# Audio tower, one core: fewer VectorE instructions in each unit, new step orders, and more hats in the first two units

## The chip, the cores and the metric
One Trainium2 chip; the program runs on one of its cores. The time is that of the device in microseconds (us), the median of several runs of one launch. Engines: TensorE (PE), VectorE (DVE), ScalarE (ACT), GpSimd (POOL) and SyncE (SP), which issues DMAs.

## The reference
128 batches of x, 750 positions by 64 channels in float32, pass three layers.
- Tokens: x is cut into 46 windows of 16 positions (taps). A product with w_off gives two offsets for each window and tap, dy and dx. With px = 16 w + k + dx, x0 = floor(px), frac = px - x0:
```
wy  = max(0, 1 - |dy|)
val = wy * ((1 - frac) * x[x0] + frac * x[x0 + 1])      # 0 outside of x
tok = val @ w_def + b_def, a class token ahead of it, + positional encoding   # 47 x 128
```
- Attention: softmax(Q K'/sqrt(128) + est) V on the layer norm of the tokens, where est = W2 tanh(W1q q + W1k k + b1) for each pair, added to the tokens.
- Experts: on the second layer norm, the two best of 8 (softmax gates, renormed) and a shared one, each relu(x w1 + b1) w2 + b2, added again. The output is 128 x 47 x 128.

## The kernel before, in words
A unit is 8 batches; there are 16. The interpolation between rows is computed in two ways. Six batches of a unit are gathered: VectorE makes row indices (stage_a, L535), GpSimd issues 36 indirect DMAs of 128 rows each into G (gathers, L367, 12 for each of three pairs of batches), and VectorE multiplies them with the weights and adds (combine, L588, pieces c0 to c2). The last two go by hats: ScalarE computes max(0, 1 - |px - row|) for all rows (hats, L402; half a batch is three Abs and one Relu; pieces h0 to h3 and k0 to k3, two to a half), TensorE multiplies this with the rows of x as they lie in memory (dense, L798, pieces n0 to n3 on TensorE) and VectorE multiplies by wy (dense_out, L618, n0 and n1 on VectorE). Both end in VT, of which TensorE makes the tokens with w_def (b3, L770).

Positions and wy of the hats must lie on all partitions. SyncE writes them to the DRAM buffer pw (write_positions, p0), reads them back spread out (spread_positions, q0: PXB and WYB), and loads the plain rows XN (load_rows, y0). It also loads x (x0, in 16 pieces), passes the estimates of the attention through DRAM into SC (e0, e1, e2) and stores the result (d9).

Each engine is a queue with an order written out by hand: ORDER lists the pieces of a step, AHEAD says which unit a letter works on. In step s the letters m and e work on unit s, r on s - 1, f, g, d (experts up, spread weights, weighted and down) on s - 2, n, c, b, k on s + 1, h on s + 2, a, p, q, y on s + 3 (offsets: a3 and a4), t and x on s + 4 (transposes of x, t0 to t3). A step ends about where stage_a writes the indices. early() runs single pieces for the units ahead of step -1; after the constants and VectorE's setup, steps -1 to 4 are unrolled, the middle is a loop of two steps, the rest is unrolled. On VectorE, chain() makes an instruction wait for the end of the one before.

Around the change: rstd (L562) takes 1/sqrt by a shifted start and three Newton steps, on 94 x 4 numbers; m6 (L656) the maximum of the scores (piece r6 in the order); m13 (L684, r13) ranks the gates by comparing all pairs; b3 on VectorE (L632) takes the tokens out of the bank to h0, for which the next unit's a3 waits, because both use bank 0. m8 (r8) adds the attention, m12 (r12) gates, m14 (r14) their weights, m51 and m52 the estimates, d8 adds up the experts, d9 transposes the output.

Of the kernel before, what the change touches and what calls it, by code (L numbers as in the profile page):

```python
# [6 lines left out]
K = 16  # L7
W = L // K
# [4 lines left out]
UNITS = B // NB  # L13
LP = 768
# [82 lines left out]
def audio_tower(nc, x, consts, rows, pw, est, out):  # L97
# [4 lines left out]
    with ctx:  # L102
# [21 lines left out]
        ones = sb("ones", [128, 128])  # L124
# [12 lines left out]
        offs = sb("offs", [128, NBLK, 8])  # L137
        nw = sb("nw", [128, NBLK, 4])
        rr = sb("rr", [128, GBLK, 4])
        e01 = sb("e01", [128, GBLK, 4, 2])  # L140
        e01f = e01[:, :, :, :].rearrange("p t n s -> p (t n s)")
        rowb = sb("rowb", [128, GBLK])
        idx = [sb(f"idx{p}", [128, GBLK * 4], i32) for p in range(2)]
        aw = [sb(f"aw{p}", [128, GBLK, 4, 2]) for p in range(2)]
# [13 lines left out]
        Z2 = [sb(f"Z2{p}", [128, COLS]) for p in range(2)]  # L158
# [13 lines left out]
        h1 = [sb(f"h1{p}", [128, COLS]) for p in range(2)]  # L172
# [8 lines left out]
        eq = sb("eq", [RT, RN, E, E])  # L181
# [20 lines left out]
        def cols(t):  # L202
# [4 lines left out]
            sem(n) for n in ("const_in", "zeroed", "psum_zeroed", "setup_psum", "setup_mats", "dve_consts"))  # L207
        blk_in, lneg_in = sem("blk_in"), sem("lneg_in")
# [8 lines left out]
        x_turned, off_full, off_ready, ot_full, ot_read, idx_ready, pw_ready = (  # L217
            sem(n) for n in ("x_turned", "off_full", "off_ready", "ot_full", "ot_read", "idx_ready", "pw_ready"))
# [16 lines left out]
        dve_chain, act_chain = sem("dve_chain"), sem("act_chain")  # L235

# [37 lines left out]
        def _(sp):  # L274
# [16 lines left out]
            def write_positions(m, h):  # L291

                u = 2 * m + h
                sp.wait_ge(pw_ready, u + 1)
                for r, t in ((0, nw[:, GBLK:NBLK, :]), (1, offs[:, GBLK:NBLK, 4:8])):
                    dst = pw[bass.ds(u, 1), r].rearrange("a (g t i n) -> t (a g) i n", g=NG, t=WG, i=32)
                    for wg in range(WG):
                        sp.dma_start(dst[wg], t[:, wg, :]).then_inc(pw_out, 16)

            def spread_positions(m, h):  # L300
# [39 lines left out]
            load_x(0, 0)  # L340
# [16 lines left out]
        def _(pool):  # L357
            pool.memset(w2blk[:, :], 0.0).then_inc(zeroed, 1)
# [5 lines left out]
            pool.memset(ones[:, :], 1.0).then_inc(zeroed, 1)  # L364
            pool.memset(mean1[:, :], 1.0 / D).then_inc(zeroed, 1)

            def gathers(m, h):  # L367
# [3 lines left out]
                for bp in range(GP):  # L371
# [683 lines left out]
```

## Time and profile before
| | us |
|---|---|
| median of 3 runs (868.21 to 872.73) | 870.32 |
| the profiled execution | 877.52 |
| its span | 875.7 |
| PE busy (80% of the span) | 698.9 |
| DVE busy (77%) | 670.8 |
| ACT busy (59%) | 515.7 |
| POOL busy (63%) | 548.8 |
| POOL: 576 gathers, 949 ns of one | 546.5 |

Each busy time is the sum over one engine's instructions. An engine that is busy for less than the span waits: for another engine, for a DMA, or between its own dependent instructions. The shares are means over a start, a loop and an end that differ. The chain of work that ended last is made of DVE 40%, PE 25%, gaps of issue 15%, ACT 7%, POOL 5%, SyncE's queue 4%.

### The profile page before, as it was taken

The numbers are of one execution on the slowest core, as the hardware profiler recorded it, in microseconds if no ns is written. First come the engines' busy times: TensorE is split into PE (matmuls) and PEld (weight loads), VectorE is DVE, ScalarE is ACT, GpSimd is POOL, SyncE is SP. The second block draws the span as 40 slices with busy tenths as digits, with TensorE's granted clock in tenths as the row PEclk, the third lists the DMA queues.
The fourth block names the chain that finished last, engine by engine and source line by source line (L and its number), as shares of the span: only waits on it lengthen the run. The fifth ranks groups of instructions, "written<-read, shape, count | busy, mean of one in ns | idle before, by whom it ended". The sixth has DMA issues, their size and how long they took to land.

```text
span 875.7 us, 18796 instructions
## 1 busy us (share of the span) xinstructions
PE 698.9 (80%) x6294; PEld 419.6 (48%) x6294; DVE 670.8 (77%) x1750; ACT 515.7 (59%) x903; POOL 548.8 (63%) x588
## 2 busy tenths in 40 slices
PE   2117586879898988888798979888898989998786
PEld 0005354545464555554454635554454556555442
DVE  5146757879888988898898878888798979795652
ACT  0307465757584857576575829576585768753522
POOL 1777777777777777777777777577675777400000
PEclk9999877899989998999999999999899999999989
DMA  5868576557473747465654657375655535200101
GB/s 145 208 147 192 93 164 126 130 94 164 76 190 57 197 71 168 104 137 131 129 140 69 191 65 182 79 141 125 122 139 73 112 55 137 50 17 11 25 1 18
DMA packets 130684, 97.98 MB, mean 112 GB/s; under 512 B 87180, under 2 KB 118868, under 8 KB 130588
## 3 DMA queue, kind: packets, MB, share of 16 engines
q0 software_dynamic: 18432, 37.79, 26.0%
q1 hardware_dynamic: 111292, 58.64, 25.8%
q8 instruction: 58, 0.95, 0.5%
q10 hardware_dynamic: 864, 0.30, 0.1%
q14 instruction: 38, 0.31, 0.1%
HBM read 88.75 MB, written 7.90 MB: 110 GB/s over the span
## 4 chain that ended last, share of the span: by engine, by line
DVE 40%; PE 25%; issue 15%; ACT 7%; POOL 5%; SPq 4%; DMA 3%; DVEq 1%; ACTq 0%; POOLq 0%
POOL G L378 5%; PE bank L936 4%; DVE bank L605 4%; DVE VAL L611 4%; PE bank L959 4%; PE bank L775 3%; DVE G L602 3%; DVE XT L531 3%; PE bank L814 3%; ACT HT L409 3%; DVE GE L724 3%; DVE VT L628 3%; PE bank L850 2%; PE bank L789 2%; DVE TH L650 2%
## 5 line engine op out<-in xcount | busy, mean ns | idle before, releaser
L378 POOL DMA_INDIRECT G<-in_x,idx x576 | 546.5, 949 | 208.5 <-issue 173.4
L409 ACT ACTIVATE HT<-PXB,c_lneg 128x736 f32<-128x736 f32 x192 | 160.1, 897 | 83.3 <-PE bank L814 64.2
L814 PE MATMUL bank<-HT,XN 128*32 128x184 f32 x3072 | 143.5, 335 | 12.8 <-issue 6.7
L936 PE MATMUL bank<-Z,c_w1e 128*128 128x376 f32 x288 | 126.9, 523 | 19.0 <-ACT HE L490 16.9
L416 ACT ACTIVATE HT<-HT 128x2208 f32<-128x2208 f32 x64 | 130.3, 2036 | 0.6
L814 PEld LDWEIGHTS bank<-HT,XN 128*32 128x32 f32 x3072 | 105.7, 115 | 50.1 <-issue 24.2
L775 PE MATMUL bank<-VT,c_wdef 128*128 128x380 f32 x256 | 89.1, 503 | 24.5 <-DVE VT L628 24.5
L959 PE MATMUL bank<-GE,c_w2e 128*128 128x376 f32 x256 | 104.0, 511 | 0.7 <-DVE GE L724 0.7
L531 DVE STREAM_TRANSPOSE XT<-xt 128x768 f32<-128x768 f32 x64 | 59.9, 958 | 52.7 <-DMA xt<-in_x 32.5
L490 ACT ACTIVATE HE<-bank,c_fb 128x376 f32<-128x376 f32 x128 | 73.0, 570 | 40.2 <-PE bank L936 38.6
L724 DVE TENSOR_TENSOR GE<-HE,bank 128x376 f32<-128x376 f32 x128 | 68.8, 538 | 35.2 <-ACT HE L490 25.5
L775 PEld LDWEIGHTS bank<-VT,c_wdef 128*128 128x128 f32 x256 | 48.9, 196 | 63.6 <-DVE VT L614 17.1
L936 PEld LDWEIGHTS bank<-Z,c_w1e 128*128 128x128 f32 x288 | 50.0, 194 | 56.6 <-ACT HE L490 30.1
L959 PEld LDWEIGHTS bank<-GE,c_w2e 128*128 128x128 f32 x256 | 45.0, 197 | 31.5 <-issue 16.3
L605 DVE TENSOR_TENSOR bank<-G,bank 128x384 f32<-128x384 f32 x96 | 54.0, 562 | 4.3 <-DVE VAL L611 1.1
L611 DVE TENSOR_TENSOR VAL<-G,bank 128x384 f32<-128x384 f32 x96 | 53.1, 553 | 3.3
L789 PE MATMUL bank<-XT,c_wof 128*32 128x384 f32 x256 | 26.5, 536 | 32.8 <-DVE XT L531 20.5
L459 ACT ACTIVATE SC<-SC,smx 47x47 f32<-47x47 f32 x128 | 40.8, 321 | 12.9 <-DVE smx L663 12.9
L614 DVE STREAM_TRANSPOSE VT<-VAL 128x768 f32<-128x768 f32 x48 | 47.0, 978 | 1.7
L602 DVE TENSOR_TENSOR G<-G,bank 128x768 f32<-128x768 f32 x48 | 45.4, 946 | 2.2 <-DMA G<-in_x,idx 1.3
L947 PE MATMUL bank<-cT,selb 72*128 72x376 bf16 x128 | 43.5, 340 | 0.3 <-DVE GE L724 0.2
L650 DVE TENSOR_TENSOR TH<-hq,bank 128x1128 f32<-128x1128 f32 (+1 forms) x32 | 40.3, 1302 | 0.6
(136 smaller groups left out, 918.7 us busy)
## 6 DMA issues: line engine op xcount, KB each, us to landing
xt<-in_x SPq DMA_DIRECT2D x256, 96.0 KB
PXB<-pw SPq DMA_DIRECT2D x16, 768.0 KB
G<-in_x,idx POOLq DMA_INDIRECT x576
XN<-in_x SPq DMA_DIRECT2D x16, 384.0 KB, 5.9
est<-SQHC SPq DMA_DIRECT2D x32, 141.0 KB
WYB<-pw SPq DMA_DIRECT2D x64, 48.0 KB
out<-OUTS SPq DMA_DIRECT2D x64, 44.0 KB
SC<-est SPq DMA_DIRECT2D x16, 69.0 KB
```

The costliest lines, as they stand in the source:

```text
L378: pool.indirect_dma_start(out=G[h][:, col, :], out_offset=None, in_=x.rearrange("b (l c) -> (b l) c", c=C), in_offset=bass.IndirectOffsetO ...
L409: act.activation(HT[half][:, c, :, :].rearrange("p g (w n) -> p g w n", n=4), PXB[h][:, :].rearrange("p (g w i n) -> p i g w n", g=NG, i=2 ...
L416: act.activation(rows_, rows_, ACT.Relu, bias=1.0, scale=-1.0).then_inc(hat_ready, 1)
L490: act.activation(HE[e % 4][:, :], cols(2), ACT.Relu, bias=cs["fb1"][:, e:e + 1]).then_inc(he_ready, 1)
L531: dve.transpose(XT[:, :, 96 * bp:96 * bp + 96].rearrange("p q (t i) -> p t q i", i=32), xt[:, WG * bp:WG * bp + WG, :].rearrange("p t (q i ...
L605: ins = dve.tensor_tensor(prod, G[h][:, k0 + a:k0 + b, C:2 * C], weight(1, a, b), ALU.mult)
L611: chain(dve.tensor_tensor(VAL[:, a:b, :], G[h][:, k0 + a:k0 + b, 0:C], prod, ALU.add))
L724: dve.tensor_tensor(GE[e % 4][:, :], HE[e % 4][:, :], cols(3), ALU.mult).then_inc(ge_ready, 1)
L775: mm = pe.matmul(bank[0][:, 0:TOK], wdef[:, q, :], VT[:, q, :], start=(q == 0), stop=(q == KP - 1))
L814: mm = pe.matmul(bank[0][32 * g:32 * g + 32, HW * c:HW * c + HW], XN[h][:, b, C * ch + 32 * c:C * ch + 32 * c + 32], HT[half][:, k, g, :], ...
L936: pe.matmul(cols(2), w1e[:, e, :], Z2[h][:, :], start=True, stop=True).then_inc(up_full, 1)
L959: pe.matmul(cols(4), w2e[:, e, :], HS[:, 0:COLS] if e == E else GE[e % 4][:, :], start=(e == E), stop=False).then_inc(down_done, 1)
```

## The change
1. stage_a on VectorE has 6 instructions behind its transpose where it had 13. The bias b_off is added by ScalarE as it copies the offsets; ScalarE gets a piece a4 (row_hats) for wy and for the two interpolation weights; their product, made in combine, replaces a copy there.
2. rstd: a start with other constants and two steps of three and four instructions in place of three of three; the factor 0.375 is put into the matrix that spreads it.
3. r6 negates its maximum in the reduction; r13 compares once, against a constant matrix of +TINY and 0, in place of twice; dense_out multiplies without the factor -1.
4. In units 0 and 1 (FULLER = 2) the third pair of batches is computed by hats and products too: GpSimd leaves 12 gathers out, VectorE the piece c2; ScalarE makes four more halves directly behind k3, TensorE four more products behind n3, VectorE two more outputs behind n1, SyncE writes, spreads and loads for them through pwx, PXE, WYE, XNE. These lie in the places of buffers that are used later only.
5. New orders on all four engines. The block a4 comes ahead of t0 to t3; n2 and n3 come late on TensorE, k2 and k3 late on ScalarE; y0 ahead of the estimates and q0 last on SyncE.
6. At the start, the first x is loaded half by SyncE and half by ScalarE, and the first constants by GpSimd.

```diff
@@ ORDER
-    "tensor": ("gc n0 fs g0 n1 m0 f0 ds f1 m1 r7 f2 g1 r8 d0 m2 g2 r9 m3 f3 g3 m4 r10 m5 f4 g4 m51 d1 r11 f5 n2 g5 m52 n3 "
-               "r12 d2 f6 g6 d3 b3 f7 g7 a3 d4 a4 d5 d6 d7 d8").split(),
-    "scalar": ("gc k0 fs r6 f0 m0 f1 r7 k1 f2 k2 m3 r9 f3 m41 m4 m5 f4 m51 k3 f5 h0 m52 h1 r12 h2 f6 h3 f7 a3").split(),
-    "vector": ("r6 c0 r7 g0 m1 g1 r8 m2 n0 g2 m3 m4 g3 r10 g4 c1 r11 g5 c2 n1 r12 r13 g6 r14 b3 g7 t0 t1 a4 d8 t2 d9 t3").split(),
-    "sync": ("x0 e0 e1 e2 p0 q0 y0 d9").split(),
+    "tensor": ("n0 fs gc g0 n1 f0 ds m0 f1 m1 r7 d0 g1 f2 r8 m2 g2 f3 m3 r9 g3 m4 d1 r10 m5 f4 m51 d2 g4 f5 m52 r11 g5 n2 "
+               "f6 r12 g6 d3 f7 g7 d4 d5 n3 d6 b3 d7 d8 a3 a4").split(),
+    "scalar": ("gc fs r6 f0 m0 k0 f1 r7 f2 k1 f3 m3 r9 m41 m4 m5 f4 m51 f5 m52 k2 f6 r12 k3 h0 h1 f7 h2 h3 a3 a4").split(),
+    "vector": ("r6 c0 r7 g0 m1 g1 r8 m2 n0 g2 m3 g3 m4 r10 g4 c1 r11 g5 r12 g6 c2 n1 r13 g7 r14 b3 d8 d9 a4 t0 t1 t2 t3").split(),
+    "sync": ("x0 y0 e0 e1 e2 p0 d9 q0").split(),
...
@@ SyncE
+                if fuller(m, h):
+                    for r, t in ((1, px[:, GBLK - WG:GBLK, :]), (0, nw[h][:, GBLK - WG:GBLK, :])):
+                        dst = pwx[u:u + 1, r].rearrange("a (g t i n) -> t (a g) i n", g=NG, t=WG, i=32)
+                        for wg in range(WG):
+                            sp.dma_start(dst[wg], t[:, wg, :]).then_inc(pwx_out, 16)
...
+                    sp.dma_start(PXE[h], pwx[u:u + 1, 1].broadcast_to([128, NG * WP * 8])).then_inc(pxx_in[h], 16)
...
+                    sp.dma_start(XNE[h], x[NB * u + GB - 2:NB * u + GB, :].rearrange(
+                        "b (p n) -> p b n", p=128)).then_inc(xnx_in[h], 16)
@@ GpSimd
+            for name, _s in CONSTS[1:NFIRST]:
+                pool.dma_start(cs[name][:, :], consts[name]).then_inc(first_in, 16)
+            pool.dma_start(ident[:, :], consts["ident"]).then_inc(ident_in, 16)
...
-                for bp in range(GP):
+                for bp in range(GP - 1 if fuller(m, h) else GP):
@@ ScalarE
+            load_first(act, (2, 3))
...
-                act.activation(off4[:, :], bank[0][:, 0:XCOLS], ACT.Copy).then_inc(off_ready, 1)
+                act.activation(off4[:, :], bank[0][:, 0:XCOLS], ACT.Identity, bias=cs["boff"][:, 0:1]).then_inc(off_ready, 1)
+
+            def row_hats(m, h):
+                u = 2 * m + h
+                act.wait_ge(ot_read, u + 1)
...
+                act.activation(nw[h][:, :, :], offT[:, :, 0:4], ACT.Abs).then_inc(nw_abs, 1)
+                act.wait_ge(nw_abs, u + 1)
+                act.wait_ge(rest_ready, u + 1)
+                act.activation(nw[h][:, :, :], nw[h][:, :, :], ACT.Relu, bias=1.0, scale=-1.0).then_inc(pw_ready, 1)
+                for i in range(2):
+                    act.activation(e01[h][:, :, :, i], rest[:, :, :], ACT.Abs, bias=float(i)).then_inc(e_abs, 1)
+                act.wait_ge(e_abs, 2 * u + 2)
+                e = e01[h][:, :, :, :].rearrange("p t n s -> p (t n s)")
+                act.activation(e, e, ACT.Relu, bias=1.0, scale=-1.0).then_inc(e_ready, 1)
@@ hats, values (ScalarE)
+                    if b == 1 and half == 1 and fuller(m, h):
+                        for bb in (2, 3):
+                            for hh in range(2):
+                                for part in hats(bb, hh):
+                                    part(m, h)
@@ VectorE, stage_a
-                chain(dve.tensor_tensor(offs[:, :, :], offT[:, :, 0:8], cs["boff"][:, :].unsqueeze(1).broadcast_to([128, NBLK, 8]), ALU.add))
-                chain(dve.tensor_tensor(offs[:, :, 4:8], offs[:, :, 4:8], base, ALU.add))
+                chain(dve.tensor_tensor(px[:, :, :], offT[:, :, 4:8], base, ALU.add))
...
+                dve.scalar_tensor_tensor(rest[:, :, :], rr[:, :, :], ROUND, pxg, ALU.subtract, ALU.subtract).then_inc(rest_ready, 1)
                 dve.wait_ge(idx_ready, u + 1)
-
-                chain(dve.scalar_tensor_tensor(nw[:, :, :], offs[:, :, 0:4], -1.0, offs[:, :, 0:4], ALU.mult, ALU.max))
-                dve.tensor_scalar(nw[:, :, :], nw[:, :, :], 1.0, 1.0, ALU.min, ALU.subtract).then_inc(pw_ready, 1)
-                dve.wait_ge(pw_ready, u + 1)
-                chain(dve.scalar_tensor_tensor(e01[:, :, :, 0], rr[:, :, :], ROUND, pxg, ALU.subtract, ALU.subtract))
-                chain(dve.tensor_scalar(e01[:, :, :, 1], e01[:, :, :, 0], 1.0, None, ALU.add))
-                chain(dve.scalar_tensor_tensor(e01f, e01f, -1.0, e01f, ALU.mult, ALU.max))
                 chain(dve.tensor_scalar(rowb[:, :], rowb[:, :], float(NB * LP), None, ALU.add))
-                chain(dve.tensor_scalar(e01f, e01f, 1.0, 1.0, ALU.min, ALU.subtract))
-                chain(dve.tensor_tensor(aw[h][:, :, :, :], e01[:, :, :, :],
-                                        nw[:, 0:GBLK, :].unsqueeze(3).broadcast_to([128, GBLK, 4, 2]), ALU.mult))
@@ VectorE, rstd
-                    for _i in range(3):
-                        chain(dve.scalar_tensor_tensor(nt_[:, :], ry[:, :], -0.5, ry[:, :], ALU.mult, ALU.mult))
-                        chain(dve.tensor_tensor(nt_[:, :], nt_[:, :], var[:, :], ALU.mult))
-                        chain(dve.scalar_tensor_tensor(ry[:, :], nt_[:, :], 1.5, ry[:, :], ALU.add, ALU.mult))
+                    chain(dve.scalar_tensor_tensor(nt_[:, :], ry[:, :], -0.703952253, ry[:, :], ALU.mult, ALU.mult))
+                    chain(dve.tensor_tensor(nt_[:, :], nt_[:, :], var[:, :], ALU.mult))
+                    chain(dve.scalar_tensor_tensor(ry[:, :], nt_[:, :], 1.68191391, ry[:, :], ALU.add, ALU.mult))
+                    chain(dve.tensor_tensor(nt_[:, :], ry[:, :], ry[:, :], ALU.mult))
+                    chain(dve.tensor_tensor(nt_[:, :], nt_[:, :], var[:, :], ALU.mult))
+                    chain(dve.scalar_tensor_tensor(nt_[:, :], nt_[:, :], -10.0 / 3.0, nt_[:, :], ALU.add, ALU.mult))
+                    chain(dve.scalar_tensor_tensor(ry[:, :], nt_[:, :], 5.0, ry[:, :], ALU.add, ALU.mult))
@@ VectorE, m6 and m13
-                chain(dve.reduce_max(smx[:, :], SC[:, :, 0:S], AX.X))
-                dve.tensor_scalar(smx[:, :], smx[:, :], -1.0, None, ALU.mult).then_inc(sc_ready, 1)
+                dve.tensor_reduce(smx[:, :], SC[:, :, 0:S], AX.X, ALU.max, negate=True).then_inc(sc_ready, 1)
...
-                chain(dve.scalar_tensor_tensor(eqv, gtv, 0.0, cs["tri"][0:RT, :].unsqueeze(1).broadcast_to([RT, RN, E * E]),
-                                               ALU.is_equal, ALU.mult))
-                chain(dve.scalar_tensor_tensor(gtv, gtv, 0.0, eqv, ALU.is_gt, ALU.add))
+                chain(dve.tensor_tensor(gtv, gtv, least[:, :].unsqueeze(1).broadcast_to([RT, RN, E * E]), ALU.is_ge))
```

## Rows read from the trace of the kernel before

**Rows 1.** by stretch: length, busy us (count) by engine (PE to POOL), clock, DMA
```profile
95.00:136.50 41.50, 28.44 (x324) 17.01 (x317) 27.57 (x64) 22.79 (x25) 31.15 (x34) 0.79 0.68 133
...
568.00:616.00 48.00, 42.53 (x395) 26.10 (x393) 41.29 (x111) 32.10 (x56) 34.13 (x36) 0.96 0.62 124
...
711.90:875.70 163.80, 140.57 (x1050) 82.71 (x1047) 112.23 (x311) 83.63 (x182) 34.11 (x36) 0.97 0.19 38
```

**Rows 2.** VectorE's timeline (start, us, engine, line): two of 16 index writes
```profile
136.39 0.20 DVE L547 TENSOR_TENSOR idx<-rr,rowb 128x36 int32<-128x36 f32 x1
...
711.96 0.20 DVE L547 TENSOR_TENSOR idx<-rr,rowb 128x36 int32<-128x36 f32 x1
```

**Rows 3.** GpSimd's timeline: first gather, one of the many, the first of unit 12
```profile
22.62 1.09 POOL L378 DMA_INDIRECT G<-in_x,idx  x1 [19.79 <-DVE idx L547]
...
59.03 0.94 POOL L378 DMA_INDIRECT G<-in_x,idx  x1 [0.30 <-issue]
...
569.35 0.94 POOL L378 DMA_INDIRECT G<-in_x,idx  x1 [5.40 <-DVE idx L547]
```

**Rows 4.** VectorE's timeline: first and last of 13 instructions in one step's index block
```profile
567.28 0.26 DVE L542 TENSOR_TENSOR offs<-offT,c_boff 128x96 f32<-128x96 f32 x1
...
570.35 0.23 DVE L559 TENSOR_TENSOR aw<-e,nw 128x72 f32<-128x72 f32 x1
```

**Rows 5.** groups by line: busy us, mean ns of one, idle before
```profile
L543 DVE TENSOR_TENSOR offs<-offs,c_base 128x48 f32<-128x48 f32 x16 | 3.3, 208 | 0.6
...
L570 DVE SCALAR_TENSOR_TENSOR nt_<-ry 94x4 f32<-94x4 f32 x96 | 15.7, 163 | 3.3
...
L692 DVE SCALAR_TENSOR_TENSOR eq<-gt,c_tri 94x256 f32<-94x256 f32 x16 | 6.9, 434 | 0.5
...
L472 ACT ACTIVATE eg<-lg 94x32 f32<-94x32 f32 x16 | 3.7, 229 | 38.5 <-DVE lg L681 38.5
```

**Rows 6.** timelines of VectorE and TensorE, from the last dense product to the offsets
```profile
602.89 0.82 DVE L628 SCALAR_TENSOR_TENSOR VT<-bank,WYB 128x184 f32<-128x184 f32 x2
...
603.77 5.37 PE L775 MATMUL bank<-VT,c_wdef 128*128 128x380 f32 x16 [1.36 <-DVE VT L628]
...
609.95 0.56 DVE L638 TENSOR_TENSOR h<-bank,pe_b 128x92 f32<-128x92 f32 x3
...
614.20 0.54 DVE L539 STREAM_TRANSPOSE offT<-bank 128x384 f32<-128x384 f32 x1
```

**Rows 7.** ScalarE's timeline, the wait at the end of a step
```profile
617.14 0.48 ACT L477 ACTIVATE cT<-bank 72x376 bf16<-72x376 bf16 x1 [4.29 <-PE bank L925]
```

**Rows 8.** timelines of ScalarE and TensorE, step -1: hats, dense and token products
```profile
75.37 2.49 ACT L409 ACTIVATE HT<-PXB,c_lneg 128x736 f32<-128x736 f32 x3
...
79.84 2.49 ACT L409 ACTIVATE HT<-PXB,c_lneg 128x736 f32<-128x736 f32 x3
...
79.99 2.08 PE L814 MATMUL bank<-HT,XN 128*32 128x184 f32 x48 [0.76 <-ACT HT L416]
...
83.90 5.34 PE L775 MATMUL bank<-VT,c_wdef 128*128 128x380 f32 x16 [1.83 <-DVE VT L628]
```

**Rows 9.** TensorE's timeline in step 0
```profile
118.56 0.66 PE L891 MATMUL bank<-TH,w2blk 128*32 128x282 f32 x8
...
123.58 7.04 PE L775 MATMUL bank<-VT,c_wdef 128*128 128x380 f32 x16 [2.35 <-DVE VT L628]
```

**Rows 10.** SyncE's timeline in the start: DMA issues
```profile
0.75 10.41 SPq L284 DMA_DIRECT2D xt<-in_x  x16
...
30.45 1.82 SPq L307 DMA_DIRECT2D WYB<-pw  x4
```

**Rows 11.** timelines of SyncE and VectorE: the estimates' stores, reading back, use
```profile
599.53 1.06 SPq L322 DMA_DIRECT2D est<-SQHC  x2
...
606.34 0.29 SPq L329 DMA_DIRECT2D SC<-est  x1
...
620.93 0.56 DVE L661 SCALAR_TENSOR_TENSOR SC<-bank,c_b2col,SC 47x376 f32<-47x376 f32 x1
```

More of the change, by code:

```diff
@@ L94, in end, with audio_tower @@
         self.base, self.n = self.outer + trips * per, 0
-def audio_tower(nc, x, consts, rows, pw, est, out):
+def audio_tower(nc, x, consts, rows, pw, pwx, est, out):
     fp32, bf16, i32 = mybir.dt.float32, mybir.dt.bfloat16, mybir.dt.int32
@@ L157, in audio_tower @@
         Z = sb("Z", [128, NB, 64])
-        Z2 = [sb(f"Z2{p}", [128, COLS]) for p in range(2)]
+        late = sb("late", [128, 2 * 2 * CH * C])
+        Z2 = [late[:, 2 * CH * C + COLS * p:2 * CH * C + COLS * p + COLS] for p in range(2)]
         var = sb("var", [RT, RN])
@@ L171, in audio_tower @@
         PT = sb("PT", [128, NB // 2, 2 * S])
-        h1 = [sb(f"h1{p}", [128, COLS]) for p in range(2)]
+        h1 = [late[:, COLS * p:COLS * p + COLS] for p in range(2)]
+        XNE = [late[:, 2 * CH * C * p:2 * CH * C * p + 2 * CH * C].rearrange("p (b n) -> p b n", b=2) for p in range(2)]
         lg = sb("lg", [RT, RN, E])
@@ L207, in audio_tower @@
             sem(n) for n in ("const_in", "zeroed", "psum_zeroed", "setup_psum", "setup_mats", "dve_consts"))
+        pwx_out = sem("pwx_out")
+        xnx_in, pxx_in, wyx_in = ([sem(f"{n}{p}") for p in range(2)] for n in ("xnx_in", "pxx_in", "wyx_in"))
         blk_in, lneg_in = sem("blk_in"), sem("lneg_in")
@@ L235, in audio_tower, with load_first, fuller, before @@
         dve_chain, act_chain = sem("dve_chain"), sem("act_chain")
+        def load_first(eng, parts):
+            for bp in parts:
+                src = x[bass.ds(2 * bp, 2), :].rearrange("b (t w g n) -> g w b t n", t=WG, w=16, g=NG)
+                for g in range(NG):
+                    eng.dma_start(xt[32 * g:32 * g + 32, WG * bp:WG * bp + WG, :], src[g]).then_inc(x_in[bp], 16)
+        def fuller(m, h):
+            return isinstance(m, int) and 2 * m + h < FULLER
+        def before(u):
+            return 4 * u + 4 * (min(u, FULLER) if isinstance(u, int) else FULLER)
         def early(engine, pieces, s):
@@ L762, in _ @@
             dve.wait_ge(dve_consts, 5)
+            chain(dve.tensor_scalar(least[:, :], cs["tri"][0:RT, :], -TINY, TINY, ALU.mult, ALU.add))
             for p in range(2):
                 chain(dve.tensor_copy(h0[p][:, :, 0:1], cls_pe[:, :].unsqueeze(1).broadcast_to([128, NB, 1])))
[L765 removed]
+            dve.wait_ge(zeroed, 9)
             steps(dve, "vector", pieces, chain, last=(UNITS - 6) // 2)
@@ L807, in piece @@
                             pe.wait_ge(ot_read, u + 2)
-                        pe.wait_ge(xn_in[h], 16 * (m + 1))
-                    pe.wait_ge(hat_ready, 4 * u + 2 * b + half + 1)
+                        if b < 2:
+                            pe.wait_ge(xn_in[h], 16 * (m + 1))
+                        else:
+                            pe.wait_ge(xnx_in[h], 16)
+                    pe.wait_ge(hat_ready, before(u) + 2 * b + half + 1)
                     for c in range(2):
@@ L814, in piece @@
                                 mm = pe.matmul(bank[0][32 * g:32 * g + 32, HW * c:HW * c + HW],
-                                               XN[h][:, b, C * ch + 32 * c:C * ch + 32 * c + 32], HT[half][:, k, g, :],
+                                               rows_[:, bb, C * ch + 32 * c:C * ch + 32 * c + 32], HT[half][:, k, g, :],
                                                start=(c == 0 and ch == 0), stop=(ch == CH - 1), skip_group_check=True)
                     mm.then_inc(dense_full, 1)
+                    if b == 1 and half == 1 and fuller(m, h):
+                        for bb in (2, 3):
+                            for hh in range(2):
+                                dense(bb, hh)(m, h)
                 return piece
```

129 lines of the change are left out of this document (84 added, 45 removed).

## Prediction

> **What bounds the kernel now.** I read the stretches first, then the times at which VectorE writes a unit's indices (this closes a step), then GpSimd's timeline, and at last one full step on VectorE and TensorE. The table by stretch [rows 1] shows in a step of the middle VectorE busy 41.3 of 48.0 us, TensorE 42.5, ScalarE 32.1. VectorE's instructions mostly wait each for the one before, so nearly all of the rest is its own gaps and a few short waits. The indices of unit 3 are written at 136.39 and those of unit 15 at 711.96 [rows 2]: 12 intervals of 47.96 us. GpSimd is not the pace there. A gather takes 0.94 us and 0.30 before it [rows 3], 1.25 us, 36 of them 45.0 us a unit. GpSimd starts at 22.62 and works without a pause until it has caught up with VectorE: unit 12 could start at 22.6 + 12 x 45 = 562.6 and starts at 569.35, after 5.40 us of waiting for its indices [rows 3]. So the loop is a chain between VectorE and TensorE; GpSimd counts in the first 110 us at most.
>
> **Steady steps.** On VectorE the block behind the offsets runs from 567.28 to 570.58 [rows 4], 13 instructions in 3.30 us. What stays is the base add, two for rr, idx, rest and rowb, six by 0.22 us (the base add takes 0.21 [rows 5]): 1.35. That is 1.95 us less. The copy of the weights into the bank becomes their product, one instruction for one, at nothing (-0.02 to +0.1, from its neighbours in these rows). Two rstd lose 2 of 12 small instructions each, 4 x 0.19 us (0.163 [rows 5] and a gap) = 0.8. The negated maximum saves 0.1 on VectorE. The dropped comparison saves 0.45 [rows 5], but it lies beside the token product of TensorE (5.37 us [rows 6]), which VectorE waits for anyway, and counts nothing in the middle. The dense product without its -1 has the same shape; nothing (-0.1 to +0.1 a call). Altogether 3.3 us less work a unit for VectorE, 2.85 of it on the path.
>
> The new lists move more than that. In the path from one transpose of the offsets to the next, VectorE's last dense product ends at 603.71, TensorE's token product runs from 603.77 to 609.14, VectorE takes its result at 609.95, and the next offsets are transposed from 614.20 to 614.74 [rows 6]: 11.0 us. VectorE comes late to the tokens (0.8 us, it is still at the experts' weights) and again some 0.3 to the offsets (behind two x transposes). The new list puts the store's two instructions into the second gap and all four x transposes behind the block, and the first lag goes with the comparison: 9.9 us, -1.1. The other part, up to the end of the dense product, gets two x transposes (+1.8) and the steps r12 and g6 (+0.9), and loses the store's two (-0.95) and the 2.85 from above: -1.1 to -1.2. Sum: -2.3 us a step, 45.7 in place of 48.0. From both sides: 44.9 if GpSimd's pace is all that holds it, 47.9 if new waits of up to 2 us, which the lists allow (r8 and m2 for the attention product, g4 for the score products), are all paid. Over 12 intervals: -27.6 us (bounds -36 and 0).
>
> ScalarE takes over five small activations a unit. That shape is not in the trace; the nearest takes 0.23 us [rows 5], so 1.2 us and two hand-overs. They stand last in its step, where it waits 4.29 us [rows 7]; their result is wanted only behind four transposes and the scores, 4.8 us later. Nothing, and 1 us a step if that cover were gone. TensorE keeps its 42.5 us of work, which fits in 45.7.
>
> **The start.** Here the change adds work to the path. One batch by hats is two halves, each of three distances and one hat: from 75.37 to 79.84, 4.47 us a half on ScalarE, while TensorE takes 2.08 for its product [rows 8]. Units 0 and 1 get two batches more, 4 halves, 17.9 us each, and these stand in ScalarE's list behind the piece k3, ahead of the token product and so of the next unit's offsets. In step -1 k3 ends at 79.9; the last hat is then ready at 97.8, the product 2.1 later, VectorE's pair 0.9 behind it. The token product starts at 100.9 where it started at 83.90 [rows 8]: +17.0. In step 0 it is worse, since k2 and k3 are moved behind m52, whose product ran at 118.56 [rows 9]: with the copy 119.7, then 4.5, 17.9, 2.1 and 0.9, so 145.1 in place of 123.58 [rows 9], +21.5. The third combine of both units falls out of VectorE and 24 gathers (30.0 us) out of GpSimd, but both wait in these stretches: unit 2's indices come at about 113, when GpSimd has stood still since 22.6 + 60 = 83, so the saved gathers buy nothing. SyncE has in unit 0 six more stores, five more spreads and one more row load ahead of the constants. Four small spreads take 1.82 [rows 10]; the second set adds 2.2 and waits some 1.3 for its own stores, the row load moved ahead gives 0.5 back: the constants and unit 2's x come 3 us later, and VectorE's setup waits for them. The split of the first x over two queues and the offsets taken ahead of the transposes may give 1 back. I take +2 (bounds -3 and +5).
>
> SyncE issues 16 pieces of x in 10.41 us [rows 10]; eight on ScalarE's queue could spare 5 us of that. The Trainium skill (DMA: Bandwidth & Descriptors, Issuing engines are not separate DMA queues) says that several issuers save only issue time, and the same page (Specifications) gives 1 us to the first byte of a DMA from GpSimd against 0.6 from the others. The first constants now come from GpSimd, where no row here shows a plain load; by the page's figures (an estimate) they would take back 0.4 us of the gain.
>
> Sum of the start: +2 + 17.0 + 21.5 - 0.6 (shorter index block) = +40. The hats are counts of rows times an order that is written in the lists. Bounds +33 and +48, the upper one if TensorE, half idle beside the hats, is granted less clock: its token product takes 5.34 us in step -1 and 7.04 in step 0, where the granted clock is 0.79 of 2.4 GHz [rows 1, 8, 9]. The Trainium skill speaks against the change here too (TensorE: Matmul & The Clock Gate, Part 1): an array that idles is clocked down and has to be warmed up again. It would add that difference, 1.7 us, to each of the two products.
>
> **The end.** Behind the last indices come 163.8 us [rows 1], four steps in which single chains decide. Two rstd, the maximum and the comparison are on them, 0.8 + 0.15 + 0.45 = 1.4 a step, less in the last: -5 (bounds -9 and -2).
>
> **Sum.** The profiled execution took 877.5 us (span 875.7), 7.2 above the median of the three runs, 870.3. 877.5 + 40 - 27.6 - 5 = 884.9; at the level of the runs 877.7, so 878 us, 0.9% slower. Within 0.5% (866.0 to 874.7) is what I call the same.
>
> **Rivals.**
> A, the loop falls further. If waits vanish with the work, the loop meets GpSimd's 45.0 us, or even goes to 44.2, which GpSimd's lead would carry through 12 units. For it: VectorE's work on the path adds up to 34.2 + 9.9 = 44.1 without any wait. Against it: TensorE would be busy 42.5 of 44.2. Times: 870.3 + 40 - 36 - 5 = 869 (the same), with 45 in place of 36 it is 860 (faster). It decides by a step under 44.7 us. The start could help it, if hats of step 0 were made while ScalarE waits (it is busy 22.8 of 41.5 us there [rows 1]).
> B, the estimates come late. SyncE's new order puts the row load, which waits for this step's last dense product, ahead of the estimates' stores. They go out at 599.53 to 600.59, the reading back at 606.34, and the scores are added at 620.93 [rows 11]. The new start is 37 us into a step; 1.8 for issues, 5.7 to land and about as much to come back makes 50.2, and they are wanted at 45.7 + 4.2 = 49.9. It decides from a loop under 46.0 us or a slower landing; 1 to 3 us a step, 12 to 36 in all: 890 to 914.
> C, the loop doesn't gain: its new waits eat the saved time (bound above). 870.3 + 40 - 5 = 905 at most, 895 in its middle.
> D, the gathers do pay: were GpSimd the pace in the start, 30 us fewer there would cover most of the hats, and the time would be 845 to 850. Against it: GpSimd would wait for indices from 83 on.
>
> **How the numbers follow.** The forecast as it stands 0.45 (own range 870 to 886, most of it slower); A 0.28, a little over half of it under 866; B 0.10; C 0.10; D 0.07. Slower: 0.36 of the forecast's 0.45, B and C, 0.56. The same: 0.08 of the forecast and 0.10 of A, 0.18. Faster: the rest, 0.26. The range leaves out D, the upper part of B and C, and the forecast's tails: 855 to 896.
>
> **What would show it.** Unit 2's indices at 110 to 117 and unit 3's at 172 to 182 (136 now), with four halves of hats without a gap on ScalarE ahead of each token product, and GpSimd idle some 30 us before unit 2: the start. Twelve intervals of 45 to 46.5 us behind them, VectorE busy about 38 us a step: the loop. If the addition of the scores waits for the estimates, it is B; if unit 3's indices come before 160, the start is wrong, and with it the sign.

## The result, and the profile after

| | before | after |
|---|---|---|
| median of 4 runs, us | 871.53 (868.21 to 874.43) | 926.83 (924.83 to 929.41) |
| ratio, 95% interval | | 1.0638 (1.0584 to 1.0691) |
| the profiled execution / its span | 877.5 / 875.7 | 929.4 / 927.6 |
| TensorE's mean granted clock in that execution (1 is 2.4 GHz) | 0.953 | 0.901 |

The change makes the kernel 6.4% slower. The sign was forecast; the time lies far outside of the range (855 to 896). The page of after, busy times and chain, and GpSimd's row:

```profile
PE 735.8 (79%) x6678; PEld 433.3 (47%) x6678; DVE 623.9 (67%) x1539; ACT 571.4 (62%) x1015; POOL 530.5 (57%) x571
...
PE 42%; DVE 23%; ACT 13%; issue 10%; DMA 6%; SPq 4%; DVEq 0%; ACTq 0%
...
L420 POOL DMA_INDIRECT G<-in_x,idx x552 | 524.7, 951 | 282.1 <-issue 164.8
```

The chain was 40% VectorE and 25% TensorE before; now it is TensorE's. I cut the span at the same places as in the prediction, at the index writes of units 3 and 15 (unit 2's stands here too). VectorE's timeline of after:

```profile
118.19 0.20 DVE L615 TENSOR_TENSOR idx<-rr,rowb 128x36 int32<-128x36 f32 x1
...
179.60 0.20 DVE L615 TENSOR_TENSOR idx<-rr,rowb 128x36 int32<-128x36 f32 x1
...
767.84 0.20 DVE L615 TENSOR_TENSOR idx<-rr,rowb 128x36 int32<-128x36 f32 x1
```

Against 136.39, 711.96 and 163.8 behind [rows 1, 2]: the start is 43.2 us longer (forecast +40), the 12 middle steps 12.7 us longer (forecast -27.6), the end 4.0 shorter (forecast -5). The sum missed by 44.5 us, and 40.3 of these are the middle. Its stretch, before, then after (length, busy us and count by engine PE, PEld, DVE, ACT, POOL, then clock, DMA):

```profile
136.39:711.96 575.57, 498.72 (x4650) 303.45 (x4639) 487.56 (x1283) 378.95 (x662) 426.28 (x449) 0.96 0.58 123
```
```profile
179.60:767.84 588.24, 514.55 (x4676) 303.29 (x4668) 459.93 (x1130) 393.64 (x722) 410.77 (x432) 0.93 0.57 118
```

By step (divide by 12): 47.96 became 49.02. VectorE fell from 40.6 to 38.3 busy, near the forecast; TensorE rose from 41.6 to 42.9 with the same products, at a lower clock. The profiled execution of after has the lowest clock and the longest time of its four: the other three ran at 0.934 to 0.939 and took 924.8 to 928.7 us.

### The profile page after: what moved, and what is told of

The parts are those of the page before. It is cut to its first block, busy times and chain, and to the rows that moved or that the text cites. A ratio compares the mean times of both kernels' runs of the same rounds, so it can differ in the third digit from the quotient of the medians.

```text
span 927.6 us, 19464 instructions
## 1 busy us (share of the span) xinstructions
PE 735.8 (79%) x6678; PEld 433.3 (47%) x6678; DVE 623.9 (67%) x1539; ACT 571.4 (62%) x1015; POOL 530.5 (57%) x571
## 4 chain that ended last, share of the span: by engine, by line
PE 42%; DVE 23%; ACT 13%; issue 10%; DMA 6%; SPq 4%; DVEq 0%; ACTq 0%
PE bank L852 8%; PE bank L1022 6%; ACT HT L470 5%; PE bank L1045 4%; PE bank L896 4%; DVE VAL L678 4%; DVE bank L672 4%; DVE G L669 3%; ACT HT L477 3%; DVE XT L597 3%; DMA SC<-est 2%; PE bank L994 2%; PE bank L866 2%; ACT SC L525 2%; PE bank L936 2%
## 5 line engine op out<-in xcount | busy, mean ns | idle before, releaser
L420 POOL DMA_INDIRECT G<-in_x,idx x552 | 524.7, 951 | 282.1 <-issue 164.8
L896 PE MATMUL bank<-HT,XN 128*32 128x184 f32 x3072 | 149.7, 346 | 32.4 <-issue 16.2
L470 ACT ACTIVATE HT<-PXB,c_lneg 128x736 f32<-128x736 f32 x192 | 159.8, 898 | 22.7 <-DMA PXB<-pw 18.7
L477 ACT ACTIVATE HT<-HT 128x2208 f32<-128x2208 f32 x72 | 146.8, 2038 | 1.4
L1022 PE MATMUL bank<-late,c_w1e 128*128 128x376 f32 x288 | 129.7, 533 | 19.8 <-ACT experts L556 18.1
L556 ACT ACTIVATE experts<-bank,c_fb 128x376 f32<-128x376 f32 x128 | 72.9, 569 | 80.6 <-PE bank L1022 70.5
L1045 PE MATMUL bank<-experts,c_w2e 128*128 128x376 f32 x256 | 105.5, 508 | 0.0
L800 DVE TENSOR_TENSOR experts<-experts,bank 128x376 f32<-128x376 f32 x128 | 69.2, 540 | 32.9 <-PE bank L1033 14.6
L1022 PEld LDWEIGHTS bank<-late,c_w1e 128*128 128x128 f32 x288 | 48.9, 197 | 63.1 <-ACT experts L556 34.1
L1045 PEld LDWEIGHTS bank<-experts,c_w2e 128*128 128x128 f32 x256 | 43.8, 193 | 23.8 <-issue 12.4
L606 DVE STREAM_TRANSPOSE offT<-bank 128x384 f32<-128x384 f32 x16 | 9.3, 583 | 62.9 <-PE bank L873 62.9
```

The costliest lines, as they stand in the source:

```text
L420: pool.indirect_dma_start(out=G[h][:, col, :], out_offset=None, in_=x.rearrange("b (l c) -> (b l) c", c=C), in_offset=bass.IndirectOffsetO ...
L470: act.activation(HT[half][:, c, :, :].rearrange("p g (w n) -> p g w n", n=4), src.rearrange("p (g w i n) -> p i g w n", g=NG, i=2, n=4)[:, ...
L477: act.activation(rows_, rows_, ACT.Relu, bias=1.0, scale=-1.0).then_inc(hat_ready, 1)
L556: act.activation(HE[e % 4][:, :], cols(2), ACT.Relu, bias=cs["fb1"][:, e:e + 1]).then_inc(he_ready, 1)
L896: mm = pe.matmul(bank[0][32 * g:32 * g + 32, HW * c:HW * c + HW], rows_[:, bb, C * ch + 32 * c:C * ch + 32 * c + 32], HT[half][:, k, g, :] ...
L1022: pe.matmul(cols(2), w1e[:, e, :], Z2[h][:, :], start=True, stop=True).then_inc(up_full, 1)
```

## The experiments

All figures of a step are means over the same 12 intervals, from the index writes of units 3 and 15 in each run's profile. Ratios are against the kernel before on the same chip. "Old orders" are ORDER of before, with a4 at the end of ScalarE's list. A step figure comes from one execution, and executions of one kernel differ: on one chip before took 871.0 to 883.5 us, which would be 1 us a step if all of it lay in the middle. Step differences of less than that are weak unless the ratios agree with them.

| run | ratio (95%) | unit 3's indices | step | unit 15's to end |
|---|---|---|---|---|
| before | | 136.4 | 47.96 | 163.7 |
| after | 1.0638 (1.0584 to 1.0691) | 179.6 | 49.02 | 159.8 |
| e1_fuller0 | 1.0193 (1.0139 to 1.0247) | 137.0 | 49.17 | 160.4 |
| e2_old_orders | 1.0102 (1.0054 to 1.0150) | 174.8 | 45.78 | 159.5 |
| e3_orders_alone | 1.0507 (1.0439 to 1.0575) | 139.1 | 51.33 | 161.2 |
| e4_pe_unrolled | 1.0480 (1.0408 to 1.0551) | 176.4 | 47.75 | 160.3 |
| e5_old_fuller0 | 0.9735 (0.9696 to 0.9775) | 136.5 | 46.07 | 161.1 |
| e6_pe_tail_mended | 1.0922 (1.0864 to 1.0980) | 182.2 | 50.82 | 161.9 |
| e7_te_se_old | 1.2718 (1.2660 to 1.2775) | 174.3 | 62.71 | 180.8 |
| e8_sync_old | 1.0585 (1.0549 to 1.0622) | 184.3 | 48.36 | 163.7 |
| e9_before_unrolled | 0.9958 (0.9916 to 1.0000) | 133.2 | 47.77 | 166.1 |
| e10_best_unrolled | 0.9640 (0.9605 to 0.9674) | 134.2 | 45.18 | 164.3 |
| f1_tails_cover | 1.0666 (1.0615 to 1.0718) | 180.3 | 49.22 | 164.4 |
| f2_tails_old | 1.0449 (1.0393 to 1.0506) | 173.9 | 47.43 | 164.6 |
| f3_hats_early | 1.1279 (1.1199 to 1.1359) | 174.4 | 53.81 | 171.3 |
| g1_gc_first | 1.0547 (1.0484 to 1.0611) | 174.3 | 48.59 | 161.9 |

**Which part costs what.** e1 leaves the extra hats out, e2 has the old orders with all the rest of the change, e3 has the new orders on the kernel before, e5 does both e1 and e2.

```diff
e1, e5:  -FULLER = 2            +FULLER = 0
e2, e5:  ORDER of before, "scalar": (... f7 a3 a4)
e3:      ORDER of after on the kernel before, without a4
```

> The changed kernel, with two batches of each unit by hats in every unit (FULLER = 0). Theory S (start): the extra hats of units 0 and 1 stand on the path, so unit 3's indices come near 137 to 140 us in place of 179.6, the loop behind them keeps its 49 us a step, and the time falls by 38 to 43 us, to 884 to 889. Rival G (the saved gathers pay): GpSimd becomes the pace with 24 gathers more, gives 30 us back, and the time falls by 12 us at most.

> The changed kernel with the four orders of the kernel before (a4 added at the end of ScalarE's). Theory O (the new orders cost the loop): with the old lists VectorE's missing work shows, the loop goes from 49.0 to 45.5 to 47.5 us a step, 18 to 42 us less, and k2 and k3 ahead of the estimates take up to 5 off the start: 880 to 905. Rival W (the instructions moved to ScalarE or the TensorE-bound loop itself hold it): the loop stays at 48.5 to 49.5, 920 to 930.

> The kernel before with the new orders alone. Theory O: TensorE's returns to the head of its loop are no longer covered (5.5 us of waiting in every second step where 3.4 partly hidden ones were), and VectorE, still with its old work, waits for the offsets: the loop takes 49.5 to 51 us a step in place of 48.0, time 890 to 910. Rival W: no change by the orders, 868 to 876.

> The changed kernel with the orders of before and with two batches by hats in every unit: what is left is less VectorE work and the new loads at the start. If the two causes add up (start 42.6 us, orders 3.2 us a step), the indices of unit 3 come near 134 to 138 us, the loop takes 45.8 us a step, and the time is 840 to 852, 3% under the kernel before. Rival G: with a loop this short GpSimd's 45.0 us a unit and its 24 gathers more hold it; the loop takes 46.5 and more, 855 to 865.

e1 puts unit 3's indices back to 137.0 and leaves the step as it is: the hats are the whole loss of the start and nothing of the loop's, as theory S had it (its time, 891, is 2 us over). e2 leaves most of the start's loss (174.8, 4.8 us earlier than after, about the 5 us expected for k2 and k3 made early) and brings the step to 45.78, 2.2 under before, which is what I had worked out for the lighter work and the new lists together. e3 has none of the lighter work and takes 51.33, 3.4 above before; this and its time (918.5) are worse than its theory said. So the lighter VectorE is worth 2.2 us a step, in the old orders (before to e2) and in the new ones (e3 to e1), and the new orders cost 3.2 (49.02 - 45.78) with it and 3.4 without it. e5 is the part of the change that pays, alone: 2.6% faster than before, inside of its forecast. That GpSimd has 24 gathers more there holds nothing up. VectorE's timeline of e5, two of its index writes:

```profile
136.46 0.20 DVE L614 TENSOR_TENSOR idx<-rr,rowb 128x36 int32<-128x36 f32 x1
...
689.31 0.20 DVE L614 TENSOR_TENSOR idx<-rr,rowb 128x36 int32<-128x36 f32 x1
```

**What the orders' 3.2 us are.** After and e2 run the same instructions in different orders. The middle of e2:

```profile
174.83:724.17 549.34, 491.66 (x4656) 300.85 (x4646) 451.23 (x1127) 388.08 (x722) 407.39 (x431) 0.96 0.63 126
```

TensorE is busy 41.0 of 45.8 us a step, against 42.9 of 49.0 in after: in these two executions 1.9 us more for the same products, at a lower granted clock (0.93 against 0.96), and 1.3 more waiting. The clock isn't the main cause, though. Two other executions of e2 ran at a mean clock of 0.924 and 0.932 and took 884.6 and 882.7 us, and three of after ran at 0.934 to 0.939 and took 925 to 929: at about the same clock the whole difference is there. The loss is also in every kind of step. At the three returns of the loop (below) after takes 53.7 us in the mean and e2 49.9; in the other nine 47.5 and 44.4; and in the five intervals of each whose clock is 1.00 throughout, none of them a return, 46.0 and 43.8.

What TensorE waited for in the middle of after, then in e2 (us in total, times, longest):

```profile
PE bank L896 <- issue: 16.2, 6, 3.4
...
PE bank L873 <- ACT off L440: 8.6, 12, 0.8
PE bank L896 <- DVE offT L606: 6.6, 9, 0.9
...
PE bank L852 <- DVE VT L702: 5.1, 12, 1.1
...
PE bank L866 <- DVE h L719: 0.8, 1, 0.8
```
```profile
PE bank L851 <- DVE VT L701: 17.4, 12, 3.7
PE bank L865 <- DVE h L718: 10.1, 12, 1.2
...
PE bank L895 <- issue: 7.2, 3, 2.7
PE bank L1010 <- issue: 3.8, 3, 1.4
```

In after the offsets' two hand-overs stand bare: a3, a4 and n0 follow each other on TensorE with nothing between, 8.6 + 6.6 = 15.2 us, 1.3 a step (the old list had d4 and the down products there, and its rows show next to none of this). And "issue", which falls on the three returns in the middle, is 16.2 us against 11.0. But e2 has waits of its own that after hardly has: 17.4 us for VectorE's last dense output and 10.1 for the tokens to be taken out of the bank, against 5.1 and 0.8. All rows of the list add up to 72 us in after and 57 in e2, so no single row is the 1.3 us; the new lists exchange some waits for others and lose by the exchange.

**The return of the loop.** The middle is a loop of two steps; steps 7, 9 and 11 begin with the jump back. After's intervals are 53.6, 54.2 and 53.3 us there and 47.5 in the mean of the other nine. TensorE's timeline at one return in after, and the same place one step later, where nothing jumps (start, us; in brackets the idle time before and what ended it); then ScalarE and VectorE behind it:

```profile
565.62 0.91 PE L873 MATMUL bank<-off,c_selm 128*128 128x384 f32 x2 [0.70 <-ACT off L440]
...
569.87 0.68 PE L896 MATMUL bank<-HT,XN 128*32 128x184 f32 x6 [3.34 <-issue]
572.80 3.84 PE L896 MATMUL bank<-HT,XN 128*32 128x184 f32 x42 [2.24 <-issue]
...
621.48 2.08 PE L896 MATMUL bank<-HT,XN 128*32 128x184 f32 x48 [0.75 <-DVE offT L606]
...
577.82 0.48 ACT L543 ACTIVATE cT<-bank 72x376 bf16<-72x376 bf16 x1 [8.69 <-issue]
...
581.33 0.20 DVE L746 RECIPROCAL sinv<-ssum 47x8 f32<-47x8 f32 x1 [3.50 <-ACT SC L525]
```

Before, the same return:

```profile
613.66 2.06 PE L959 MATMUL bank<-GE,c_w2e 128*128 128x376 f32 x6
...
616.75 0.35 PE L925 MATMUL bank<-identb,c 94*72 94x94 bf16 x4 [0.88 <-issue]
...
619.77 3.90 PE L814 MATMUL bank<-HT,XN 128*32 128x184 f32 x45 [2.20 <-issue]
```

In after the wait comes in two parts, 3.34 and 2.24 us, and the 42 products behind it take 3.84 us where 48 took 2.08. Before, down products ran until 615.9 and the parts were 0.88 and 2.20; in after nothing is queued ahead of n0, and gc, for which ScalarE waits, stands behind n0. e4, e9 and e10 write TensorE's loop out (after, before, e5); g1 moves gc to the head.

```diff
e4, e9, e10:
-            steps(pe, "tensor", pieces)
+            for s in range(-1, UNITS + 2):
+                for name in ORDER["tensor"]:
+                    v = s + AHEAD[name[0]]
+                    if 0 <= v < UNITS:
+                        pieces[name](v // 2, v % 2)
g1, tensor:  -n0 fs gc g0 n1        +gc n0 fs g0 n1
```

> The changed kernel with TensorE's loop written out, the other engines as they are. Theory L (return to the loop's head): the three waits of 3.3 and 2.2 us on TensorE at the steps of units 10, 12 and 14 go, with the low clock behind them, and those steps fall from 53.7 to 46 to 50 us: 12 to 23 us less, 904 to 915. Rival P: such waits come from TensorE's rate of taking up 96 short products and weight loads and move elsewhere, 922 to 930.

> The kernel before with TensorE's loop written out. If the down products and VectorE's own work cover the return in the kernel before, as its steps of 50.8, 50.6 and 49.8 us against 46 to 48 leave open, it gains 3 to 7 us: 866 to 870. If they don't cover it at all, 10 us: 862 to 865.

> As the run with the orders of before and no extra hats, and TensorE's loop written out. Theory L: its steps at the returns (50.2, 50.4 and 49.1 us with the old orders) fall to 45 to 46, 10 to 14 us less: 828 to 842. Rival P: under 4 us, since the down products cover part of it already.

> The changed kernel with one piece moved on TensorE: gc (the transposes of the experts' weights) ahead of n0 again. Theory K: ScalarE's list begins with gc, and all that stands behind it (the exponentials, then VectorE's softmax) waits when n0 is late at the return to the loop's head; gc ahead takes 2 to 4 us off the steps of units 10, 12 and 14 and under 0.5 off the others: 6 to 15 us less than the changed kernel. Rival: the low clock and the late n0 itself make those steps long, under 4 us.

Written out, after gains 1.3 us a step, and all of it at the returns (steps 7, 9, 11: 47.4, 49.0, 48.8; the other nine 47.5 as in after), with ratios whose intervals lie apart: theory L. e5 gains 0.9, the intervals apart as well, but in time 1.0%, short of the 10 to 14 us expected. The kernel before gains 0.2 in the profile and 0.4% in time, an interval that ends at no change. g1 gains 0.4 a step and as much again in the start: by the intervals it is a small gain or none. By these profiles the return costs most where TensorE's list is the new one, less in the old one with a lighter VectorE, and least before, where VectorE was the busier.

**The ends of the lists.** e6 mends TensorE's list alone, f1 adds VectorE's a4 ahead of the stores, f2 takes VectorE's old end.

```diff
e6, f1, f2 tensor: -n0 fs gc g0 ... f7 g7 d4 d5 n3 d6 b3 d7 d8 a3 a4
                   +gc n0 fs g0 ... f7 g7 n3 b3 a3 d4 a4 d5 d6 d7 d8
vector:            -b3 d8 d9 a4 t0 t1 t2 t3
f1:                +b3 a4 d8 d9 t0 t1 t2 t3
f2:                +b3 t0 t1 a4 d8 t2 d9 t3
```

> The changed kernel, in TensorE's new order only gc put first again and the down products d4 to d8 put behind a3 and a4 as before. Theory T (TensorE's list lost its cover): the return to the loop's head costs 2 to 4 us less and the waits for the offsets are filled again, the loop goes from 49.0 to 46 to 47.5 us a step, 890 to 915. Rival V (VectorE's list, with its four transposes behind the block and no work while the offsets are made): 48.5 to 49 a step, 920 to 930.

> TensorE's new list with gc first and d4 to d8 behind a3 and a4, as in the run that had only this, and VectorE's a4 now ahead of d8 and d9, so that its sum of the experts no longer stands ahead of the offsets. Theory I (the lists interlock: there the 64 us of waiting for d8 made the loss): the wait goes, the loop comes to 46 to 48 us a step in place of 50.8, 885 to 910. Rival Q (the tail isn't where the new lists lose): 49 and more, over 920.

> The same with VectorE's end of the step wholly as before: b3 t0 t1 a4 d8 t2 d9 t3. Theory I: as good as the run before or better by the two transposes that fill the wait for the offsets, about 1 us a step, 880 to 900. Rival Q: over 920.

All three missed: e6 is slower, not faster; f1 came out at 935 us, as its rival Q had it; f2 at 911, better than its rival and short of its theory. VectorE's waits in e6 (whole run), then in the middle of f1:

```profile
DVE HS L804 <- PE bank L1049: 64.2, 14, 5.3
```
```profile
DVE offT L605 <- PE bank L872: 39.3, 12, 3.3
```

VectorE still has d8 ahead of its index block, and d8 now waits 4.6 us each time for the down products that I had put behind a3 and a4. With a4 ahead of it (f1) that is gone, but VectorE now waits 3.3 us a step for the offsets, with nothing to do meanwhile, and the step is no better than after's. With two x transposes ahead of a4 as well (f2) that wait has no row left (one of 1.6 us a step for a bank ahead of the transposes comes in), and the step falls to 47.43, 1.6 under after; this is 1.8 us under f1, a difference that the ratios (1.0449 and 1.0666) bear out. What TensorE waits for in the middle of f2, the row that e2 lacks:

```profile
PE bank L895 <- ACT HT L476: 14.7, 12, 2.7
```

The 14.7 us for hats, 1.2 a step, have no row in e2's waits: the new lists make k2 and k3 late on ScalarE, and n3 waits for them. It is about as long as the 1.3 us a step by which TensorE idles more in f2 than in e2. f3 tried to show it, with ScalarE's old list and n2, n3 around m52:

```diff
f3 tensor: -f5 m52 r11 g5 n2 f6 ... d4 d5 n3 d6 b3
           +f5 n2 m52 n3 r11 g5 f6 ... d4 d5 d6 b3
   scalar: as in e2
```

> The changed kernel with only the hats and their products put where they were within the middle of a step (ScalarE's list of before with a4 at its end, n2 ahead of m52 and n3 behind it on TensorE). Theory M (late hats hold the token product): loop 46.5 to 48, 890 to 910, and the start shortened by up to 4 us. Rival: hats are ready early enough anyway, the loop stays at 49 within 0.5.

> The changed kernel with TensorE's and ScalarE's orders of before (a4 added at ScalarE's end), VectorE's and SyncE's as changed. Theory T: nearly all of what the old orders give comes back, loop 45.5 to 46.5, 882 to 895. Rival V: less than half of it, loop over 47.4, 905 and more.

Both missed widely. e7 takes TensorE's and ScalarE's old lists beside VectorE's new one: 62.7 us a step. VectorE's waits in e7, one row:

```profile
DVE experts L799 <- ACT experts L555: 174.1, 53, 8.6
```

VectorE stands 174 us at pieces of g whose input ScalarE hasn't made yet, and, as in e6, another 80 us at d8, for down products that TensorE's old list makes only behind a3 and a4. The lists lock into each other, so a list of one engine put back or mended alone measures the mismatch, not the list. That the late hats cost 1.2 us is read from f2's waits and not shown by a run that removes them.

**SyncE.** e8 has SyncE's old list ("x0 e0 e1 e2 p0 q0 y0 d9").

> The changed kernel with SyncE's order of before. Theory B (the estimates come late, because the row load stands ahead of their stores): 0.5 to 1.5 us a step come back, 905 to 920. Rival: nothing, since TensorE holds the loop, 922 to 930 (at this chip's level of the kernel before).

0.5% in time with overlapping intervals. The profile shows 0.7 us a step less, but the start and the end are 4.7 and 3.9 us longer, and the whole isn't shorter: its rival has it. Also in after VectorE adds the scores at 626.24 without a wait, and SyncE had read the estimates back at 618.63. Rival B did not happen.

## Why the prediction was right or wrong

**The start: right.** Forecast +40, measured +43.2. Timelines of ScalarE (last of the extra hats), TensorE (setup, a product beside the hats, the two token products) and SyncE in the start of after:

```profile
102.17 2.04 ACT L477 ACTIVATE HT<-HT 128x2208 f32<-128x2208 f32 x1
...
71.12 0.77 PE L1070 MATMUL bank<-c_wk,c_wq 128*128 128x128 f32 x2 [19.74 <-DVE b2s L833]
...
95.32 3.88 PE L896 MATMUL bank<-HT,late 128*32 128x184 f32 x48 [1.65 <-ACT HT L477]
...
107.49 5.37 PE L852 MATMUL bank<-VT,c_wdef 128*128 128x380 f32 x16 [1.14 <-DVEq L709]
...
168.90 5.37 PE L852 MATMUL bank<-VT,c_wdef 128*128 128x380 f32 x16 [1.17 <-DVEq L709]
...
35.43 0.35 SPq L339 DMA_DIRECT2D experts<-pwx  x1
...
38.48 0.42 SPq L385 DMA_DIRECT2D c_wdef<-in_wdef  x1
```

The setup before:

```profile
64.74 0.77 PE L984 MATMUL bank<-c_wk,c_wq 128*128 128x128 f32 x2 [18.47 <-DVE b2s L757]
```

The four halves run without a gap ahead of each token product, as counted. Unit 2's indices come at 118.2 (just outside of the 110 to 117 forecast), unit 3's at 179.6 (172 to 182). The missed 3 us are the setup: SyncE reaches the constants at 38.48 behind the second set of stores and spreads, and TensorE's setup begins at 71.12, 6.4 later than before where I took 2 (my bound was 5). From there the first token product starts 17.2 later than before (17.0 forecast), and the second another 21.7 (21.5). 1.7 us of this come back, since both token products take 5.37 us, at full clock: the 7.04 of before [rows 9] did not come again, and my upper bound for it wasn't needed. Beside the hats the clock did fall (48 products took 3.88 us at 95.32 and 2.08 at 104.27), but it was up again at both token products. I had no reason for that, so it is luck that these 1.7 us cover a part of the setup's 4.4. The start is also less firm than 3 us: the runs with the extra hats have unit 3's indices between 173.9 (f2) and 184.3 us (e8).

**The gathers buy nothing: right.** GpSimd's timeline of after:

```profile
119.29 0.94 POOL L420 DMA_INDIRECT G<-in_x,idx  x1 [35.38 <-DVE idx L615]
...
180.69 0.94 POOL L420 DMA_INDIRECT G<-in_x,idx  x1 [16.75 <-DVE idx L615]
```

Idle 35.4 us before unit 2 (some 30 forecast): rival D is out. e1 and e5, with all the gathers back, have unit 3's indices at 137.0 and 136.5 us.

**The end: right**, -4.0 for -5.

**VectorE's lighter work: nearly right in size.** 3.3 us a unit less work, 2.85 on the path were forecast; in e2 VectorE is busy 3.0 us a step less and the step is 2.2 shorter. Whether the five activations on ScalarE take part of the other 0.65 no run separates. Rival A did not come in after, but it wasn't empty: e2's nine steps outside of the returns take 44.4 us in the mean, the 44 to 45 that A had, in the old orders.

**The failed step: "The new lists move more than that ... Sum: -2.3 us a step, 45.7 in place of 48.0 ... Over 12 intervals: -27.6 us."** The measured term is +12.7. The forecast's -2.3 a step is the lighter work, -2.85, and some +0.6 for the new lists (-1.1 at the tokens and offsets, +1.8 and +0.9 and -0.95 before them). Measured, the lighter work is -2.18 a step (e2), -26.2 in all, and the lists are +3.24 (after against e2), +38.9 in all. So the term that failed is the price of the new lists: it makes 32 of the 40 us missed in the loop, the lighter work 8. Three things were wrong in it.

First, I followed one path, VectorE's from transpose to transpose, and gave TensorE a single line: "keeps its 42.5 us of work, which fits in 45.7". It fits only in the clean steps, those with neither a return nor a low clock, which take 45.6 to 46.4 us; in the others TensorE is busy for up to 46.2 us, and its own gaps come on top. Stretches of after, a step with the return, one without it, and an earlier pair (the first has low clock and no return):

```profile
276.30:326.50 50.20, 45.92 (x405) 27.09 (x397) 38.94 (x96) 33.24 (x61) 34.74 (x37) 0.90 0.56 120
326.50:372.10 45.60, 41.20 (x394) 24.00 (x390) 38.57 (x96) 33.14 (x61) 33.89 (x36) 1.00 0.69 128
567.90:622.10 54.20, 46.19 (x409) 27.22 (x413) 38.90 (x96) 33.35 (x61) 34.45 (x36) 0.91 0.50 110
622.10:668.10 46.00, 40.82 (x385) 23.68 (x374) 38.70 (x96) 33.13 (x61) 34.20 (x36) 1.00 0.65 128
```

Behind the last dense product the tokens and offsets take 10.0 us for my 9.9 in such a step (token product from 657.28, offsets turned at 667.28). Half of the steps are not like that: with a lower clock or the loop's return they take 48.7 to 54.2.

Second, the base was a mean over both kinds. A clean step of before:

```profile
372.30:418.90 46.60, 40.99 (x394) 24.46 (x392) 40.97 (x108) 31.99 (x56) 35.14 (x38) 1.00 0.59 130
```

46.6, not 48.0; before's four clean intervals take 46.2 in the mean. After's five take 46.0, so its clean step is only 0.2 us shorter, in spite of the lighter work. In e2 they take 43.8: the old lists with the lighter work gain 2.4 us in clean steps too. From 46.2 my -2.3 would have given 43.9, so it is luck that the 45.7 of the forecast nearly meets after's clean step.

Third, I asked of TensorE's new end only where VectorE is late, not what TensorE does in a3, a4 and n0 without anything between (1.3 us a step of waiting by the rows above, partly paid for by shorter waits elsewhere), and took "new waits of up to 2 us" as the worst, with no loss as the end of the range. The loop could lose, and did.

Rival C (new waits eat the gain) had the right direction and too small a price: up to 905 where 927 came.

**What stays open.** Which place in the lists costs how much: e4 shows the return's part (1.3 us a step in after, 0.9 in e5) and f2 that of the ends and gc together (1.6); no run takes the rest apart. Also why the clock falls within a step. Five-microsecond stretches of the first step above:

```profile
286.00:291.00 5.00, 4.37 (x16) 2.87 (x15) 3.71 (x16) 3.17 (x7) 3.77 (x5) 0.58 0.89 282
291.00:296.00 5.00, 5.00 (x44) 3.07 (x44) 2.33 (x5) 2.69 (x3) 3.78 (x5) 0.50 0.96 226
```

From about 287 to 296 TensorE runs at 1.2 GHz, though it had been busy 4.43 and 4.04 of 5 us at 2.4 GHz in the two stretches before, and no loop returns there. That the new lists bring more of this isn't shown. The profile of f2 has 0.97 and 41.4 us busy a step, after's 0.93 and 42.9, but over whole executions f2 ran at 0.915 to 0.952 and after at 0.901 to 0.939; and within one kernel the times go with the clock by about 1% (f2: 909.5 at 0.952, 919.2 at 0.915).

## What to carry to other kernels

When the work of the leading engine is cut, work out the path of the next one as closely, its hand-overs and its gaps at the loop's return included, and take as the base a step of one kind rather than a mean over several. Before a clock or a wait is called the cause, look at the other executions, and at the waits of the faster kernel too. A new order and less work are two changes: time each without the other (here -2.2 and +3.2 us a step), and put the orders of all engines back together, since one alone can cost more than all. e10, the lighter VectorE in the old orders, no extra hats and TensorE's loop written out, takes 842.7 us, 3.6% under the kernel before and just above its forecast (828 to 842); its index writes on VectorE:

```profile
134.23 0.20 DVE L614 TENSOR_TENSOR idx<-rr,rowb 128x36 int32<-128x36 f32 x1
...
676.41 0.20 DVE L614 TENSOR_TENSOR idx<-rr,rowb 128x36 int32<-128x36 f32 x1
```

## What the runs showed of the hardware

- A loop's return on TensorE: two waits of 3.34 and 2.24 us in after, 0.88 and 2.20 in before, the second in the middle of a block, after six products (after) and three (before), and half clock behind them (42 products in 3.84 us, 48 in 2.08 elsewhere). Where work was queued ahead of the jump, only the first part was shorter. The Trainium skill (Runtime: NRT & Kernel Launch, Instruction fetch mechanics) says that a taken branch out of the fetched window stalls the engine and that kernels therefore prefer to be unrolled. That e4, e10 and, within its interval, e9 are faster agrees; that these waits are fetches no run shows.
- Beside the hats TensorE had about 2 us of products in each 4.5, and its clock went down and up (48 products in 3.88 us at 95.32, in 2.08 at 104.27); the token products behind them ran at full clock (5.37 us twice), where before one took 7.04 at the same place [rows 9].
- The mean clock of whole executions of one kernel differed (after 0.901 to 0.939, e2 0.924 to 0.963) with little effect on the time: e2 took 882.7 us at 0.932 and 891.9 at 0.950.
